# A two-layer vision tower with experts in fp32: GpSimd's indirect transfers without pauses, and more of the first expert stage's gathers moved into the second attention

## The reference

```python
h = patches_mlp(x)                                   # 16x16 patches, silu, second matrix
h = h + attention0(layernorm(h))                     # 16 heads of 64, causal, plus its own residual
h = h + experts0(layernorm(h))                       # one shared expert and the 2 best of 7
h = h + attention1(layernorm(h))                     # compressed q, k, v with gelu and rotary parts
h = h + experts1(layernorm(h))                       # the 4 best of 16
...
# experts0, of one token x:
xt = silu(x @ sh_gate) * (x @ sh_up) @ sh_down
top_p, top_i = top_k(sigmoid(x @ w_r + b_r + routing_bias), 2)
out = xt + sum(top_p[k] / sum(top_p) * expert[top_i[k]](x))
```

## Time and profile before

| | |
|---|---|
| median of three runs | 1585.34 us (1579.11 to 1585.96) |
| the profiled execution | 1588.56 us |
| its span | 1586.7 us |
| PE busy | 1388.1 us, 87% |
| DVE busy | 1047.5 us, 66% |
| ACT busy | 758.5 us, 48% |
| POOL busy | 634.1 us, 40% |
| mean granted clock of PE | 0.926 |

### The profile page before, as it was taken

The page is one execution under the profiler, slowest core; times in us unless marked ns, Lnnn a source line. Parts: engine busy times, 40 slices in busy tenths (PEclk is TensorE's granted clock), DMA queues, the critical chain, the costliest instruction groups (busy, mean ns, idle before and its releaser), DMA issues. The chain is left out here.

```text
span 1586.7 us, 37038 instructions
## 1 busy us (share of the span) xinstructions
PE 1388.1 (87%) x14188; PEld 1219.2 (77%) x14188; DVE 1047.5 (66%) x2196; ACT 758.5 (48%) x1288; POOL 634.1 (40%) x608
## 2 busy tenths in 40 slices
PE   6979999999999987768994588889976889999995
PEld 5867888888888877768994466667756889999994
DVE  4744674674674675876566567888776876666775
ACT  5433444444444442334553366767742346666641
POOL 4005422112112002535627255333336757663765
PEclk9999999999999998889997788999975899999997
DMA  8304664243353104225865000000008248888963
GB/s 287 119 26 152 220 210 147 88 160 116 105 174 134 55 2 156 103 96 172 250 196 161 6 28 28 2 1 2 2 1 318 104 163 253 266 273 255 280 214 111
DMA packets 142883, 215.57 MB, mean 136 GB/s; under 512 B 14336, under 2 KB 112768, under 8 KB 141824
## 3 DMA queue, kind: packets, MB, share of 16 engines
q1 hardware_dynamic: 121648, 160.20, 30.4%
q0 software_dynamic: 18624, 52.45, 10.5%
q10 hardware_dynamic: 2448, 0.61, 0.2%
HBM read 103.64 MB, written 109.58 MB: 134 GB/s over the span
## 5 line engine op out<-in xcount | busy, mean ns | idle before, releaser
L125 PE MATMUL e_p_gu<-e_w_hi,e_xt_hi 128*128 (+1 forms) x676 | 200.8, 297 | 12.9 <-DVE e_xt_lo L723 9.6
L125 PE MATMUL e_p_gu<-e_w_hi,e_xt_lo 128*128 (+1 forms) x676 | 195.0, 288 | 0.0
L125 PE MATMUL e_p_gu<-e_w_lo,e_xt_hi 128*128 (+1 forms) x676 | 194.9, 288 | 0.0
L125 PEld LDWEIGHTS e_p_gu<-e_w_hi,e_xt_hi 128*128 128x128 f32 x676 | 132.9, 197 | 15.1 <-issue 12.8
L1271 POOL DMA_INDIRECT e_xn<-results,e_row_of x112 | 115.6, 1032 | 62.6 <-issue 28.9
L125 PEld LDWEIGHTS e_p_gu<-e_w_lo,e_xt_hi 128*128 128x128 f32 x676 | 133.3, 197 | 0.0
L125 PEld LDWEIGHTS e_p_gu<-e_w_hi,e_xt_lo 128*128 128x128 f32 x676 | 133.2, 197 | 0.0
L125 PE MATMUL e_p_y<-e_w_hi,e_hid_hi 128*128 (+1 forms) x338 | 110.9, 328 | 8.9 <-DVE e_hid_lo L742 7.0
L1254 POOL DMA_INDIRECT rows<-e_xn,e_row_of x96 | 95.5, 995 | 52.9 <-issue 28.7
L1938 DVE TENSOR_TENSOR a_ot_lo<-a_O,a_ot_hi 128x1024 fp32r<-128x1024 f32 x32 | 39.1, 1223 | 115.3 <-ACT a_ot_hi L1881 115.3
L125 PE MATMUL a_J<-a_xt_hi,w_qk_hi 128*128 128x512 f32 x256 | 106.6, 417 | 8.3 <-DVE a_xt_lo L1956 6.3
(11 more groups left out here) (335 smaller groups left out, 4374.4 us busy)
## 6 DMA issues: line engine op xcount, KB each, us to landing
e_moved<-rows SPq DMA_DIRECT2D x121, 256.0 KB, 3.2
results<-e_y SPq DMA_DIRECT2D x121, 256.0 KB
rows<-a_zero SPq DMA_DIRECT2D x28, 1024.0 KB, 5.8
pa_x<-in_x SPq DMA_DIRECT2D x7, 1536.0 KB, 6.5
w_qk_in<-in_we SPq DMA_DIRECT2D x24, 384.0 KB, 6.3
we_parts<-w_qk_in SPq DMA_DIRECT2D x24, 384.0 KB, 2.5
we_parts<-a_e_lo SPq DMA_DIRECT2D x24, 384.0 KB, 2.4
e_w_hi<-we_parts SPq DMA_DIRECT2D x4, 1536.0 KB, 16.1
```

The lines of the kernel that those rows point to most:

```text
L125: mm = eng.matmul(out, lhs[a], rhs[b], start=start and n == 0, stop=stop and n == len(terms) - 1, skip_group_check=skip)
```

## The change

1. `rest()` is gone everywhere: no clearing and no wait between indirect transfers, in both expert stages.
2. The first expert stage gathers and combines blocks 0 to 15 only (`LATE_FROM = 16`). Blocks 16 to 31 are gathered in the second attention, in four parts of four blocks: POOL issues 8 transfers in each of tiles 0 to 3 into two buffers by turns (of the same total size as the one before), and DVE adds a part in the tile after, in two pieces of four operations, then one of statistics, then an empty one.
3. The roots are taken in smaller lots. The one for blocks 0 to 7 and the normalised first tile lie inside the expert loop (ACT at step 46, DVE at step 47). The one for blocks 8 to 15 is requested at the stage's end and taken by ACT behind its first copy in the attention. Each late part has one of its own, ACT's at the ends of tiles 1 to 4, DVE's inversion one tile later.
4. The five transfers of constants go from ACT's queue to SP's; DVE takes the low part of the first turned tile (`turned_low(0)`) before it normalises the second; POOL's loop over pairs of tiles is written out.

```diff
-BURST = 2
+FIRST0, LATE_FROM = 8, 16
...
-    def first_rows(self, dve):
+    def first_rows(self, dve, blocks=EARLY):
-        self.invert(dve, self.EARLY)
+        self.invert(dve, blocks)
         normalise(dve, self.core, self.core.xn0, 0)
...
@@ shared_phase
+    first_done = plan.chunk_end[0] + combine_step(0, FIRST0 // 2 - 1)
-    groups = [(c, first) for c, (low, high) in enumerate(chunks) for first in range(low, high, 2)]
+    groups = [(c, first) for c, (low, high) in enumerate(chunks) for first in range(low, min(high, LATE_FROM), 2)]
...
-                        if (n * top_k + k) % BURST == BURST - 1:
-                            rest()
...
-                        if c == 0 and k % BURST == BURST - 1:
-                            rest()
...
-            norm.root(act, norm.EARLY)
+                if s == first_done + 1:
+                    norm.root(act, (0, FIRST0))
...
             def finish(g):
                 combine(g)
-                if groups[g][1] + 2 == norm.SPLIT:
-                    dve.wait_ge(stats, 3 * (TILES - 2))
-                    norm.request(dve, norm.EARLY)
+                done = groups[g][1] + 2
+                if done in (FIRST0, LATE_FROM):
+                    dve.wait_ge(stats, 3 * (done // CH))
+                    norm.request(dve, (0, FIRST0) if done == FIRST0 else (FIRST0, LATE_FROM))
...
+                if s == first_done + 2:
+                    norm.first_rows(dve, (0, FIRST0))
...
-            norm.first_rows(dve)
...
+    return Late(tables, [(n, n + CH) for n in range(LATE_FROM, BLOCKS, CH)], top_k, row_of, weight, stores)
...
@@ attention1_phase
-        late_rows = sb("late_rows", [P, late.chunk[1] - late.chunk[0], late.k, D])
+        late_rows = [sb(f"late_rows{i}", [P, CH, late.k, D]) for i in range(2)]
...
+        @block.sync
+        def _(sp):
+            for dst, src in ((bias, "bias1"), (head_mask, "head_mask"), (cos, "cos"), (sin, "sin")):
+                sp.dma_start(dst[:], d[src]).then_inc(c_in, 16)
+            sp.dma_start(bo[:], d["bo"].partition_broadcast(P)).then_inc(c_in, 16)
...
-            def late_gather(n):
+            def late_gather(part, n):
+                table, rows = late.tables[n]
+                if part >= 2 and n == late.parts[part][0]:
+                    pool.wait_ge(late_added, late.k * (part - 1))
...
-                    few = late.chunk[0] + CH * u if is_first(t2) else None
+                    few = late.parts[t][0] if t < len(late.parts) else None
...
-                    if t == 3:
-                        norm.root(act, norm.LATE)
+                    if 1 <= t <= len(late.parts):
+                        norm.root(act, late.parts[t - 1])
             turned_high(0)
+            norm.root(act, (FIRST0, LATE_FROM))
...
             def add_late():
-                low, high = late.chunk
-                dve.wait_ge(late_in, 16 * late.k * (high - low))
...
+                for part, (low, high) in enumerate(late.parts):
+                    dve.wait_ge(late_in[part % 2], 16 * late.k * CH * (part // 2 + 1))
+                    for k in range(late.k):
+                        if k > 0:
+                            dve.wait_ge(late_added, part * late.k + k)
+                        for n in range(low, high):
+                            row = core.h[:, n, :]
+                            last = dve.scalar_tensor_tensor(row, late_rows[part % 2][:, n - low, k, :], late.weight[:, n, k:k + 1], row,
+                                                            ALU.mult, ALU.add)
+                        last.then_inc(late_added, 1)
+                        yield
...
-            normalise(dve, core, xn, 1).then_inc(xn_done, 1)
...
             turned_low(0)
+            normalise(dve, core, xn, 1).then_inc(xn_done, 1)
```

More of the change, by code:

```diff
@@ L447 @@
 class Late:
-    results: object
-    rows: int
-    chunk: tuple
+    tables: dict
+    parts: list
     k: int
@@ L538, in shared_phase @@
         expert_at = sb("expert_at", [1, len(chunks), room], mybir.dt.int32)
-        idle = sb("idle", [P, 16])
         st = sb("st", [P, CH, DVE_BN])
@@ L613, in _ @@
             core.clear_spent(pool)
-            cleared = Chain(pool, rested)
-            def rest():
-                cleared(pool.memset(idle[:], 0.0))
             def scatter(c):
@@ L848, in combine @@
                     last.then_inc(combined if k == top_k - 1 else rounds, 1)
-                if (first + 2) % CH == 0 and first + 2 <= norm.SPLIT:
+                if (first + 2) % CH == 0:
                     hold(dve, combined, g + 1)
@@ L1006, in shared_phase @@
     stores = [(y_stored[i], 16 * sum(x % STORES == i for x in range(len(plan.of_move)))) for i in range(STORES)]
-    return Late(d["results0"][-1][0:rooms[-1] * P], rooms[-1] * P, chunks[-1], top_k, row_of, weight, stores)
+    tables = {n: (d["results0"][c][0:rooms[c] * P], rooms[c] * P) for c, (low, high) in enumerate(chunks) for n in range(low, high)}
+    return Late(tables, [(n, n + CH) for n in range(LATE_FROM, BLOCKS, CH)], top_k, row_of, weight, stores)
 class Flow:
@@ L1132, in sorted_phase @@
         list_at = [sb(f"list_at{c}", [1, rooms[c]], mybir.dt.int32) for c in range(len(chunks))]
-        idle = core.bias[0][0]
         st = sb("st", [P, CH, DVE_BN])
@@ L2265, in _ @@
             probabilities(0, 0)
-            looped(pool, TILES // 2, pair)
+            for t2 in range(TILES // 2):
+                pair(t2, last=t2 == TILES // 2 - 1)
         @block.scalar
         def _(act):
-            for dst, src in ((cos, "cos"), (sin, "sin"), (head_mask, "head_mask"), (bias, "bias1")):
-                act.dma_start(dst[:], d[src]).then_inc(c_in, 16)
-            act.dma_start(bo[:], d["bo"].partition_broadcast(P)).then_inc(c_in, 16)
             def turned_high(n):
```

48 lines of the change are left out of this document (19 added, 29 removed).

## The result

The changed kernel takes 1572.27 us (median of 7 runs, 1565.41 to 1577.0), the kernel before beside it 1582.41 (7 runs). The ratio is 0.9933, with an interval of 0.9909 to 0.9958: 4 to 9 per thousand faster. The forecast was 1574.7. The profiled execution took 1574.9 us with a span of 1573.1, against 1588.56 and 1586.7.

The account below looks back on a forecast made before the run. PE was taken as the bound nearly everywhere, so its standstills count. Terms -22.1 - 4.5 - 1.0 + 17 = -10.6 took the profiled 1588.56 to 1578.0, or 1574.7 us for the median; range 1566 to 1583, for 8 in 10 1561 to 1587.

Parts of the forecast that it names:

- The stage change: End of the first expert stage: PE starts the attention at 856.8 instead of 878.94, -22.1 us (-21 to -23).
- The loop: First expert stage: pauses removed from scatters and gather 0, less the new root and normalising, -4.5 us (-7.2 to +1.7).
- The wait on the store behind scatter 1: First expert stage: ACT waits 3.73 us for a free e_y; scatter 1 without pauses gives PE 3.3 us.
- the root and the first tile in the loop: First expert stage: ACT's table loads cost 1.3 us on PE's path, DVE's normalising of that tile 0.5.
- The attention's start: Second attention: DVE takes the low part at once, before normalising the second tile, -1.0 us.
- The tiles: Second attention: DVE's late work, two more tiles with gathers and three more roots cost +17 us (6 to 27).
- The additions: Second attention: late pieces, part of DVE's 12.1 us of added work, of which 0.88 reaches the time, +10.6.
- The gathers: Second attention: eight transfers on POOL cost 3.1 us a tile, for two more tiles +6.2.
- The second expert stage: Pauses of gather 0 there are covered by the next gather's 16.95 us wait for stored results: 0 (-1 to +2).
- The slower one: Attention: nine added small DVE operations each wait 2.3 us for POOL, +20.8, median 1595.5 us; chance 0.07.
- The attention gives all back: Second attention costs its upper bound, +27 us, for a median of 1584.7; chance 0.25.
- the late work hides: Second attention costs only +6 us as pieces fill DVE's idle time, for a median of 1563.7; chance 0.15.

Follow-up runs that it names:

- changed_late24: The changed kernel with LATE_FROM = 24, so blocks 16 to 23 are gathered and combined in the first expert stage again: 1577.18 us, ratio 0.996.
- before_no_pauses: The kernel before with every pause between GpSimd's indirect transfers taken out and nothing else changed: 1578.61 us, ratio 0.9966.

## Why the prediction was right, and where it was off

**The stage change (-22.1).** Nearly right in size: -23.3, and right that POOL's rate over the gathers sets the gap (changed_late24). Wrong was the link behind it. I read the last combine, the root and the normalised tile as what ends the stage, and 1.56 us as the barrier's own. It was POOL's drain that ended it, 1.2 us later than DVE; the barrier itself takes 0.3, and that is all that is left of the 1.56 once DVE comes last.

**The loop (-4.5).** Right, though the first pair of traces seemed to deny it (+0.1): 5.3 by the means, and 5 us of time by two pairs of kernels, of which one is clear of the noise. The wait on the store behind scatter 1 went entirely. The one on the first combine is 1.4 us or less in the twelve traces without pauses, where I had none. The 1.8 us for the root and the first tile in the loop weren't found.

**The attention's start (-1.0).** PE's first wait became 1.3 us shorter, near the forecast; the other 2.1 of the -3.4 are not tied to the change. "The constants come from SP's queue, so 0" was wrong: once DVE's order no longer covered the queue, it was worth 0.95 at that wait. I had costed two edits one at a time against the old order, where each hides the other.

**The tiles (+17).** Right in sum, 12.9 to 18.1 over the seven traces with the changed kernel's tiles, and in shape. Its terms were not right. The additions pass about half of their time on (4.9 of 9.8) and not 0.88. The gathers cost two thirds of the forecast, 6.4 for three quarters of them where 9.3 were expected. What the sum did not have at all is the `mv` and the place of the gathers: 3 us and 9 us come back when POOL's operations are put in another order, with the same work in them. I had taken the gathers' cost as one of time on POOL; it is largely one of place, and it reaches the time mostly through PE's clock.

**The second expert stage (0).** Right.

**The sum.** That the median came within 2.4 us of the forecast is partly luck. In the pair of traces it stands against, the loop missed by 4.6 us one way, and the attention's start, its tiles and the stage change by 6.3 us the other way, and both contain differences that come and go between executions of one program.

**The rivals.** The slower one had its mechanism half right. Small operations do stand behind POOL's addition, but none of the nine that the change added does; three of the stage's ordinary seven `mv` do, at 2.3 us each, of which 3 us came back in the distances, and one of the three stood so before the change. What I held against this rival, that the late pieces of 1.66 show none of it, was no evidence: in none of the fourteen traces does a late piece run beside an arithmetic operation of POOL; they stand where POOL waits or issues transfers. "The attention gives all back" (+27) and "the late work hides" (+6) both failed: the whole attention grew by 10.5, the mean of four traces of the changed kernel's attention (320.6, 317.6, 317.0, 322.9) less that of two of the old (310.6, 307.4).

## What to carry to other kernels

Here, work that was moved from a stage's end into a stage that is near balance was paid again at about half its price (10.5 of 23.3 us), and how much depended less on how long it is than on what it stands ahead of in its queue. So when transfers are spread over another engine's work, try them behind the operation that others wait for, in the longest gap between two such operations, even in a row of four. At a stage's end, ask of every engine when it signs off, not only of the one whose work ends last in the timeline. And measure a claim of a few microseconds on the stretch between two instructions in several traces: the first pair of traces here denied a gain of 5 us that was there, and it showed 3.4 us at the attention's start, of which 1.3 are tied to the change.

## What was not expected of the hardware

A DVE operation of 128x8 numbers that takes 0.17 us took 2.4 to 2.7 us whenever POOL's addition of 128x1024 started about when it did (from 0.05 us before it to 0.33 behind it), in every one of the traces with the old place of the addition. Where it began in the addition's last 0.15 us, as in every later tile, it kept its 0.17 or 0.18, and the statistics of four times 128x256 kept their 1.40 beside the whole addition. It is not a matter of small operations. The normalising is hit as well, at the attention's start of the kernel before, where one of its operations, 0.40 elsewhere, takes as long as POOL's clearing (1.80) beside it:

```profile
878.94 1.90 DVE L420 TENSOR_SCALAR a_xn<-h,mv,rstd 128x256 f32<-128x256 f32 x1 [1.56 <-PEq L514]
...
878.89 1.80 POOL L2206 MEMSET a_vz<- 128x2048 f32 x1 [9.54 <-POOLq L514]
```

That is why the normalising that DVE did first took 4.43 us and not 1.4.

POOL signs off from a stage 8.2 to 9.3 us after its last indirect transfer ends: 9.3 in the three traces with all of gather 1 (the kernel before, before_no_pauses, changed_late24), 8.2 in the nine of the shorter one in which the `DRAIN` is recorded. And the same program differs from trace to trace by up to 4 us within one stage of 230 us, with PE's granted clock at 0.50 or 1.00 in the same five microseconds of the program.
